# The lengths of keys and queries move to the front of VectorE's half step

## The reference

```
for each of 2 depths:
    h = shift_token(x)                     # the right half of the columns comes from the token before
    q, k, v = split(h @ wqkv)
    q = q / max(norm(q), 1e-12) * q_scale  # norm over the 64 columns of a head
    k = k / max(norm(k), 1e-12) * k_scale
    q, k = rotary_xpos(q, k)
    x = x + local_attention(8 * q, k, v) @ wo      # windows of 64 tokens
    h = layernorm(shift_token(x)) * lg + lb
    a, g = split(h @ w1 + b1)
    x = x + (a * gelu(g)) @ w2 + b2
```

## Time and profile before

| | us |
|---|---|
| median of 3 runs | 5179.33 |
| lowest and highest | 5178.75, 5185.25 |
| the profiled execution | 5168.04 |
| its span | 5166.7 |
| the gate of the second layer in it, about | 1160 to 1625 |

### The profile page before, as it was taken

How to read it: one execution, slowest core, us unless ns; L and a number is a source line. 1 busy time by engine, 2 the same in 40 slices (tenths; PEclk the granted TensorE clock), 3 DMA queues, 4 the chain that set the end, 5 groups by cost and what they waited for, 6 DMA issues and landing times. The chain is left out here.

```text
span 5166.7 us, 68811 instructions
## 1 busy us (share of the span) xinstructions
PE 4541.0 (88%) x27376; PEld 2213.2 (43%) x27376; DVE 3154.0 (61%) x4176; ACT 2497.4 (48%) x3813; POOL 2316.0 (45%) x1323
## 2 busy tenths in 40 slices
PE   5999999987886777868799999987799999999997
PEld 3444444445654333323322222223455555555554
DVE  4656565636666777762377777844465655566563
ACT  2344444446663555542256666651244444444443
POOL 0455555558771677870100000000166666666674
PEclk8999999989997999989799999997899999999998
DMA  0000000011110000000000000000000000000000
GB/s 32 3 3 3 3 3 3 3 33 29 37 26 12 2 2 2 1 1 23 3 2 2 1 2 1 1 3 6 10 3 3 3 1 3 3 3 1 3 1 9
DMA packets 61954, 36.81 MB, mean 7 GB/s; under 512 B 36308, under 2 KB 53888, under 8 KB 61376
## 3 DMA queue, kind: packets, MB, share of 16 engines
q1 hardware_dynamic: 61632, 32.41, 2.5%
HBM read 22.03 MB, written 1.05 MB: 4 GB/s over the span
## 5 line engine op out<-in xcount | busy, mean ns | idle before, releaser
L793 DVE TENSOR_REDUCE L_part<-banks 128x2 f32<-128x1024 f32 (+2 forms) x1600 | 1882.2, 1190 | 988.1 <-PE banks L644 847.7
L778 ACT ACTIVATE L_weights<-banks 128x1024 f32<-128x1024 f32 (+1 forms) x1600 | 1579.8, 1000 | 1048.3 <-PE banks L676 835.6
L702 PE MATMUL banks<-L_weights,L_V 128*32 128x512 f32 (+3 forms) x6400 | 1497.3, 603 | 5.6 <-ACT L_weights L778 3.6
L1000 POOL TENSOR_TENSOR L_wsum<-L_wsum,L_weights 128x1024 f32<-128x1024 f32 (+1 forms) x448 | 983.4, 2195 | 55.8 <-ACT L_weights L778 3.1
L983 POOL TENSOR_TENSOR L_wsum<-L_wsum,L_two 128x1024 f32<-128x1024 f32 x240 | 570.3, 2376 | 854.9 <-DVE L_two L967 852.6
L702 PEld LDWEIGHTS banks<-L_weights,L_V 128*64 128x64 f32 (+1 forms) x6400 | 283.3, 123 | 459.4 <-issue 396.9
L676 PE MATMUL banks<-L_QH,L_KH 64*128 64x512 f32 (+3 forms) x1664 | 431.7, 453 | 18.1 <-issue 10.2
L2510 POOL MEMSET F_xr<- 128x16 f32 x1 | 0.1, 126 | 934.6 <-POOLq L97 934.6
L644 PE MATMUL banks<-L_KH,L_QH 64*128 64x512 f32 (+3 forms) x1664 | 371.1, 428 | 31.6 <-ACT L_weights L778 17.5
L676 PE MATMUL banks<-L_QL,L_KH 64*128 64x512 f32 (+3 forms) x1664 | 371.8, 382 | 0.0
L676 PE MATMUL banks<-L_QM,L_onesrow 64*128 64x512 f32 (+3 forms) x1664 | 371.1, 380 | 0.0
(11 more groups left out here) (446 smaller groups left out, 5914.3 us busy)
## 6 DMA issues: line engine op xcount, KB each, us to landing
F_early<-F_V SPq DMA_DIRECT2D x63, 128.0 KB, 2.3
F_tab<-xpos SPq DMA_DIRECT2D x8, 512.0 KB, 4.5
F_h<-L_ffn_h_w SPq DMA_DIRECT2D x2, 1024.0 KB, 8.1
F_wqkv<-L_ffn_wqkv SPq DMA_DIRECT2D x2, 768.0 KB
L_cos<-rope_cos SPq DMA_DIRECT2D x1, 1024.0 KB, 5.0
L_sin<-rope_sin SPq DMA_DIRECT2D x1, 1024.0 KB, 7.0
out<-X SPq DMA_DIRECT2D x1, 1024.0 KB, 5.1
F_z<-F_x SPq DMA_DIRECT2D x32, 31.8 KB
```

The lines of the kernel that those rows point to most:

```text
L702: mm = pe.e.matmul(O[r, c:BANK], self.V[g % 2][:, kt, h, :], self.W[x % self.NW][:, y, c:BANK], start=kt < starts, stop=kt >= tiles - starts)
L778: act.e.activation(self.W[x % self.NW][:, :, c:BANK], self.banks(it)[:, :, c:BANK], ACT.Exp, scale=self.scale).then_inc(self.exped, 1)
L793: dve.e.tensor_reduce(self.part[n % 3][:, pr, j, p, :], self.banks(it)[:, :, 0:wide], AX.X, ALU.max).then_inc(self.mx_read, 1)
L1000: pool.e.tensor_tensor(acc[:, :, c:BANK], acc[:, :, c:BANK], W[:, :, c:BANK], ALU.add).then_inc(self.summed, 1)
```

## The change

One number of the table `rank` changes: `lengths` goes from 4 to 1. Within its half step it then stands ahead of `layernorm`, `join` and `shift` (still 4, in their old order) and behind `turn`, which has none in that half step. Nothing is added or removed.

```
-        rank = {"turn": 0, "stats": 0, "moments": 1, "table": 3, "join": 4, "shift": 4, "layernorm": 4, "lengths": 4, "zturn": 4, ...}
+        rank = {"turn": 0, "stats": 0, "moments": 1, "table": 3, "join": 4, "shift": 4, "layernorm": 4, "lengths": 1, "zturn": 4, ...}
```

More of the change, by code:

```diff
@@ L1613, in plan @@
             put(first + 14, ("down", u))
-        rank = {"turn": 0, "stats": 0, "moments": 1, "table": 3, "join": 4, "shift": 4, "layernorm": 4, "lengths": 4, "zturn": 4, "turnx": 5, "gate": 5, "spin": 6, "qkv": 7, "up": 8, "down": 8, "norm": 10, "root": 10}
+        rank = {"turn": 0, "stats": 0, "moments": 1, "table": 3, "join": 4, "shift": 4, "layernorm": 4, "lengths": 1, "zturn": 4, "turnx": 5, "gate": 5, "spin": 6, "qkv": 7, "up": 8, "down": 8, "norm": 10, "root": 10}
         items = self.items = []
```

## The result

| | before | after |
|---|---|---|
| median, us | 5175.97 (19 runs, 5163.61 to 5187.58) | 5188.29 (19 runs, 5177.27 to 5199.31) |
| ratio, 95% interval | | 1.0025 (1.0017 to 1.0034) |
| profiled execution, us | 5168.04 | 5197.33 |
| ScalarE starts the SiLU that closes the gate, us | 1622.16 | 1635.54 |

The changed kernel is slower by 0.25%, about 13 us (9 to 18). The forecast was 18.5 us. The two profiled executions differ by 29, but single executions of one kernel scatter by some 10 us to either side, so the totals of two profiles are a poor measure here. The gate itself is a better one: in the profile its first projection starts at 1160.70 before and at 1161.21 after, and its last step starts 13.4 us later. So the gate lasts 461.5 us before and 474.3 after, 12.9 more. The other 16 us between the two profiles lie outside the gate, in stages that the change doesn't touch.

The account below looks back on a forecast made before the run. TensorE, busy 88% of the span, was taken as pace maker. Units summed 5 x 3.3 + 2.3 - 0.3 = 18.5 us longer; 5179.3 + 18.5 = 5197.8, given as 5197 us, range 5168 to 5212.

Parts of the forecast that it names:

- rival 2: Layer norm beside GpSimd: some L2061 pass between GpSimd's instructions, L1763 1 to 2 us late; 5 to 10 us more; chance 0.23.
- The move with VectorE's durations unchanged: Units 2 to 7: spin and norm paths both bring L1763 2.45 us earlier; with unit 1's 0.43, some 15 us gained.
- TensorE's clock may add to this: TensorE around L1763: keeping its clock could raise the uncontended gain from 15 us to up to 25 us.
- Contention: VectorE's layer norm beside GpSimd's earlier spin: each instruction waits until the running GpSimd instruction ends; L1763 3.3 us later.
- The signs named for it: Profile after: L2103 wait about 4.2 us, L1829 wait 8 to 9, L1763 wait gone, L2055 to L2058 0.7 or more, four L2061 4 to 5.
- One wait for each of eight instructions: L2055 to L2058 and four L2061 each wait for one GpSimd instruction; L1829's idle time goes from 0.72 to 8.7 us.
- the two places named in the bounds: GpSimd's pauses between dependent instructions, where a VectorE one may slip in, saving 0.72 and 1.26 us; part of the lower bound.
- the upper bound: GpSimd is in turn held up by each of the eight, 2.0 us: L1763 5.3 us late, sum about 31 us.
- The sum: Gate over all units: 5 x 3.3 + 2.3 - 0.3 = 18.5 us longer.
- TensorE's clock, costed at nothing: Half clock falls behind L1829 instead of L1763; costed at nothing, bounded by some 3 us of work per unit either way.
- the forecast's steps around L1763: TensorE starts L1829 at 1325.9, works 3.04 us, then starts L1763 at 1328.9, 3.3 us later than before.
- The backlog on VectorE, costed at nothing: Score maximum and ScalarE's exponentials come some 6 us later, covered by up to 6.9 us idle before L1881; costed at nothing.

Follow-up runs that it names:

- GpSimd held: Changed kernel, but GpSimd's first spin of keys in units 2 to 7 also waits for the normed tiles; ratio to the kernel before 0.998, again 0.9976.
- the kernel with both moves: Changed kernel with the sum of x ahead of the layer norm and L1829 a half step later; 5185.42 us, ratio 1.0030 to the kernel before.
- the kernel with only the sum in front: Changed kernel with VectorE's order lengths, sum of x, layer norm; 5183.32 us against 5166.31 for the kernel before, ratio 1.0034.

## Why the prediction was right

The forecast was 5197 us on the median, and 5188 was measured. 3.4 of the 9 us are the median of the kernel before, which was 5179.33 in three runs and 5175.97 in nineteen. The rest is in the sum: 12 to 13 us were lost and not 18.5. That lies between the forecast and its rival 2 (5 to 10 us), and the range of 5168 to 5212 was wide enough to hold no change at all. So it is the signs in the profile that speak for the mechanism, more than the total does.

*The move with VectorE's durations unchanged* (both paths 2.45 us earlier). Not tested by any run: none has the lengths in front, GpSimd free to start and the layer norm unblocked. With GpSimd held the gate is 13 to 15 us shorter, near the 15 of that sum, but this is coincidence. There the spin starts 0.36 us earlier in the half step and not 2.45, and the gain comes behind L1763, at full clock. The prediction had that term only as a remark (TensorE's clock may add to this).

*Contention.* Right in kind. The signs named for it are all there: GpSimd's wait before L2103 is 4.16 us where about 4.2 was said, L1829 waits 7.97 (8 to 9 said), TensorE's wait before L1763 is gone in units 2 to 7, and four L2061 take 4.38 (4 to 5 said). One sign was off: L2057 and L2058 with 0.58 and 0.64 us stay under the 0.7 named, since a blocked instruction lasts only what is left of GpSimd's, and GpSimd's L2105 and L2106 have 0.72. The summary of the per tile norm for all units:

```profile
L2061 DVE TENSOR_SCALAR F_z<-F_z,F_mv,F_rstd x32: 337/1077/1419, 1266.2 to 1620.3; 128x128 f32<-128x128 f32 x32
```

*One wait for each of eight instructions.* The term was too large by one. L2056 slipped through the pause, seven waits remained, and L1829's wait was 7.97 instead of 8.7. This was one of the two places named in the bounds; at the other, between L2107 and L2108, none got through. The condition of the upper bound, a GpSimd held up in its turn, did not come about.

*The sum.* The idle times before L1829 and L1763, taken together for each unit, are before 1.72 + 4.69 (unit 2), 0.72 + 4.69 (units 3 to 6) and 0.89 + 5.74 (unit 7). After, they are 9.98, four times 7.97, and 8.14. So the units lost 3.6, 4 x 2.56 and 1.5, together 15.3, where the forecast had 5 x 3.3 + 2.3 = 18.8. Unit 1 gained more than 0.3: the L1763 of its second tile starts at 1235.36 instead of 1236.38, with the gate's start 0.5 later, so 1.5. (That gain isn't firm. With GpSimd held nothing differs in unit 1, and the same instruction came 0.2 us later than before in one profile and 1.6 earlier in the other.) That is 13.8 us, beside 13.4 - 0.5 = 12.9 at the gate's end and a median 12.3 higher. The term that was mis-sized is the wait per unit, 2.56 for 3.3.

*TensorE's clock, costed at nothing.* The place of the half clock moved as said. Behind L1829 it is granted 0.50, and behind L1763 1.00; the earlier trace rows had it the other way round:

```profile
1327.50:1329.00 1.50, 1.50 (x5) 1.18 (x6) 1.50 (x3) 0.41 (x1) 1.50 (x2) 0.50 0.02 4
1332.20:1335.00 2.80, 2.80 (x31) 2.75 (x26) 2.63 (x4) 2.71 (x9) 2.72 (x3) 1.00 0.40 94
```

Over the gate TensorE's busy time stayed at 376.4 us, so the two cancel and nothing was the right price for this kernel. But the forecast's steps around L1763 cancel too. The 3.04 us of work between L1829 and L1763 took 1332.25 - 1327.44 = 4.81, so L1763 came 4.3 us later in its half step and not 3.3; and the 31 matmuls from L1763 on took 5.52 us where they took 8.20. It isn't a price of nothing in general: with GpSimd held, the place of the half clock made the gain. No experiment changed the clock alone, so its part is read from the rows of two orders that shift it.

*The backlog on VectorE, costed at nothing.* Right for this kernel: ScalarE's wait before L1881 fell from 44.5 to 17.0 us, the cover being used up, and TensorE's time is accounted for without it. But it was hidden only under L1829's wait. In the kernel with both moves that wait was gone and the backlog came out as waits at L1820 and in the exponentials.

What isn't settled: why the kernel with both moves has a median 19 us above before when its gate is 8 us longer. One candidate is the kernel before: beside this kernel its median was 5166.31, and 5175.56 to 5176.31 in the three other groups of runs. Against 5176 the kernel with both moves would be 9 us above, which fits its gate; but the kernel with only the sum in front, from the same group, would then be 7 above, with a gate 15 us longer. Also open is how much of the differences of 2 to 5 us between the medians is real, and what the early spin would be worth with a layer norm that nothing blocks.

## What to carry to other kernels

Before an instruction on VectorE is moved, look at what GpSimd will be doing beside it at the new time: an early start of GpSimd makes nearly every short VectorE instruction from SBUF to SBUF that comes up then (here `tensor_tensor`, `scalar_tensor_tensor`, `tensor_scalar` and `copy`) as long as the rest of the running GpSimd instruction, so the number of instructions counts and not their size. Reciprocals were not blocked: L2034 kept its 0.55 us in all eight units, as beside L2108 in unit 2 of the changed kernel, at 1260.83. Put first the many short ones, then what releases GpSimd, and behind that what was never blocked here, such as L1970 with its input in PSUM. Where that can't be, holding GpSimd back for 2 us was worth more (-10 us) than letting it start (+13 us). And where TensorE must wait twice in a row, look at where its half clock falls: ahead of a wait for another engine it costs little, behind that wait it costs its full time.

## What was not expected of the hardware

- A VectorE instruction gets through a pause of 0.08 us between two GpSimd instructions that depend on each other: L2056 kept its 0.16 us in all six layer norms that came up beside GpSimd's spin (the last two of the eight have no spin beside them), here in one row. With the sum of x in front, L2056 took 0.64 us, and it was L2058 that kept its 0.16, started between the end of L2107 and the start of L2108:

```profile
L2056 DVE TENSOR_TENSOR F_rb<-F_rb,F_ra x8: 161/161/163, 1264.7 to 1618.9; 128x4 f32<-128x4 f32 x8
```

- A shorter idle time in two pieces was followed by another clock than a long one. After 4.69 us of idle before L1763 the granted clock was 0.50. With GpSimd held, 2.96 us of idle stand before L1829 and 0.52 before L1763, and the clock was 0.63 over the work behind the first and 1.00 behind the second (the rows under that experiment).

- An activation of ScalarE on 128x128 values in SBUF with scale and bias per partition took 0.478 us, and VectorE's norm of the same tile 0.34 when GpSimd stood still.
